# Loads and PSUM banks of the embedding start in a two-layer language-model tower

## Time and profile before

| | |
|---|---|
| Median of 3 runs | 4845.25 us (4837.85 to 4854.96) |
| Profiled execution, its own time | 4843.86 us |
| Its span | 4842.1 us |
| Mean granted TensorE clock | 0.96 of full |
| Busy share PE, DVE, ACT, POOL | 90%, 70%, 49%, 66% |

### The profile page before, as it was taken

How to read it: one execution, slowest core, us unless ns; L and a number is a source line. 1 busy time by engine, 2 the same in 40 slices (tenths; PEclk the granted TensorE clock), 3 DMA queues, 4 the chain that set the end, 5 groups by cost and what they waited for, 6 DMA issues and landing times. The chain is left out here.

```text
span 4842.1 us, 62755 instructions
## 1 busy us (share of the span) xinstructions
PE 4357.8 (90%) x17088; PEld 2261.8 (47%) x17088; DVE 3396.1 (70%) x5016; ACT 2378.6 (49%) x4078; POOL 3186.6 (66%) x1637
## 2 busy tenths in 40 slices
PE   6999986997899999999999999999999975999994
PEld 4666654664333333343433334343333333666673
DVE  4766673111799999999999999999999985111114
ACT  2555542222566665656666565666656534221221
POOL 2222212441799999999999999999999961444441
PEclk9999997998899999999999999999999987999997
DMA  1000012342223232323233333223323221333456
GB/s 31 20 23 20 20 49 60 112 126 73 97 100 106 102 106 99 105 99 104 100 105 103 101 105 100 102 100 108 105 103 105 96 76 38 103 117 112 125 167 219
DMA packets 262442, 453.11 MB, mean 94 GB/s; under 512 B 38892, under 2 KB 175932, under 8 KB 262300
## 3 DMA queue, kind: packets, MB, share of 16 engines
q1 hardware_dynamic: 238876, 403.66, 25.5%
q0 software_dynamic: 23424, 48.00, 3.2%
HBM read 409.75 MB, written 41.81 MB: 93 GB/s over the span
## 5 line engine op out<-in xcount | busy, mean ns | idle before, releaser
L1745 POOL TENSOR_TENSOR m_xh<-m_u,m_Bb 128x1536 f32<-128x1536 f32 x512 | 1752.1, 3452 | 220.2 <-DVE m_u L1619 220.2
L1674 PE MATMUL bank<-m_xh,ident 128*128 128x512 f32 x3072 | 1442.7, 605 | 25.2 <-POOL m_xh L1734 25.2
L1701 ACT ACTIVATE bank<-m_dt,m_Ac 128x508 f32<-128x508 f32 x1536 | 1019.2, 683 | 419.3 <-DVE bank L1716 283.6
L1716 DVE TENSOR_TENSOR_SCAN bank<-bank,m_xh 128x512 f32<-128x512 f32 x864 | 1060.1, 1227 | 36.3 <-ACT bank L1701 7.8
L1674 PEld LDWEIGHTS bank<-m_xh,ident 128*128 128x128 f32 x3072 | 567.7, 191 | 804.9 <-issue 732.6
L1716 DVE TENSOR_TENSOR_SCAN m_xh<-bank,m_xh 128x512 f32<-128x512 f32 x672 | 774.2, 1204 | 31.6 <-ACT bank L1701 27.3
L1734 POOL TENSOR_TENSOR m_xh<-m_xh,m_Cb 128x1536 f32<-128x1536 f32 x224 | 773.1, 3452 | 11.7 <-DVE m_xh L1716 11.3
L1725 DVE TENSOR_TENSOR m_xh<-bank,m_Cb 128x512 f32<-128x512 f32 x864 | 597.7, 692 | 70.0 <-DMA m_Cb<-BC_rows 24.9
L1184 ACT ACTIVATE f1t_h<-bank,f1t_b 128x512 f32<-128x512 f32 (+1 forms) x276 | 147.9, 587 | 509.9 <-PE bank L1214 491.1
L1533 PE MATMUL bank<-m_xp,m_dg 128*128 128x512 f32 x768 | 349.8, 598 | 3.3 <-ACT m_xc L1541 2.6
L1114 POOL DMA_INDIRECT rows_y<-f1t_y,f1t_home x142 | 140.1, 987 | 317.4 <-DVE f1t_y L1155 288.1
(11 more groups left out here) (366 smaller groups left out, 6142.6 us busy)
## 6 DMA issues: line engine op xcount, KB each, us to landing
m_Bb<-BC_rows SPq DMA_DIRECT2D x256, 512.0 KB, 4.7
m_Cb<-BC_rows SPq DMA_DIRECT2D x256, 512.0 KB, 3.9
f1t_w<-f_w SPq DMA_DIRECT2D x46, 576.0 KB
f1t_w1a<-f_w SPq DMA_DIRECT2D x46, 384.0 KB
f0t_w<-f_w SPq DMA_DIRECT2D x22, 576.0 KB
f1c_yg<-rows_y SPq DMA_DIRECT2D x16, 768.0 KB, 8.2
f1t_w1b<-f_w SPq DMA_DIRECT2D x92, 96.0 KB
f0t_w1a<-f_w SPq DMA_DIRECT2D x22, 384.0 KB
```

The source lines that it names most:

```text
L1674: mm = pe.matmul(bank[:, c, :], K.ident[:, :], xh[n % NX][:, c, :], start=False, stop=(d == 1 and n == NS - 1))
L1701: act.activation(o[:, :, lo:hi], seqs(dt[d][:, c, :])[:, :, lo:hi], ACT.Exp, scale=Ac[:, c, n:n + 1]).then_inc(s_dA, 1)
L1716: dve.tensor_tensor_scan(o, bank[:, 3 + p % 3, way], xh[n % NX][:, c, way], 0.0, ALU.mult, ALU.add).then_inc(s_h, 1)
L1745: pool.tensor_tensor(xh[n % NX][:, :, :], u[d][:, :, :], Bb[q % RB][:, n % QN, :].unsqueeze(1).to_broadcast([P, DC, TOK]), ALU.mult).then_ ...
```

## The change

Only the start of `attention_phase` is changed, and only for group 0; groups 1 to 15 keep their waits and bank 7.

- SP no longer waits for POOL in the load block. It issues `ids_w`, the three id rows of group 0 and the three tables, seven DMAs, each kind with a semaphore of its own, and waits for none of them. The id rows were issued in the main block before.
- The other 11 loads (gamma, beta and all weights) are issued by ACT at the beginning of the main block.
- The waits stand at the users: POOL's index copy waits for `ids_w`; PE's `emb0` for the tables; POOL's gamma step and PE's `q0` for all 11 weights.
- DVE sets the `V` tiles after the one-hots of group 0 instead of in the load block; ACT's first copy into `V` waits for it.
- The nine front steps of group 0 go to five banks (`BANKS`), and PE's waits between `emb0` and `emb1`, between `zT0` and `zT1` and between `q0` and `q4` are gone. Because banks 0 to 3 are among them, the first scores wait for the copies of all five of `q0` to `q4`.

```diff
+        WEIGHTS = (
+            (gam[:, :], ...), (bet[:, :], ...), (wqp_a ...), (wqp_b ...), (wqp_b bias ...),
+            (wq_a ...), (wq_b ...), (wq_b bias ...), (wo_a ...), (wo_b ...), (wo_b bias ...),
+        )
+        BANKS = {"emb0": 7, "emb1": 0, "zT0": 1, "zT1": 2, "q0": 3, "q1": 7, "q2": 0, "q3": 1, "q4": 2}
+        front = lambda g, name: BANKS[name] if isinstance(g, int) and g == 0 else FB
...
             @block.vector
             def _(dve):
-                for v in V:
-                    dve.memset(v[:, :, :, :], 0.0).then_inc(s_V, 1)
-                dve.wait_ge(s_V, 2)
-                for v in V:
-                    dve.memset(v[:, :, :, HD:HD + 1], 1.0)
...
             @block.sync
             def _(sp):
-                n = 0
-                sp.wait_ge(cleared, 4)
-                for dst, src in (
...
-                    (wo_b[CR:CR + 1, :], A["bproj"]), (ids_w[:, :], A["ids_wordT"]),
-                ):
-                    sp.dma_start(dst, src).then_inc(loaded, 16)
-                    n += 1
-                sp.wait_ge(loaded, 16 * n)
+                sp.dma_start(ids_w[:, :], A["ids_wordT"]).then_inc(s_idw, 16)
+                ids_front(sp, 0)
+                for dst, src in ((posi_t[:, :], A["posi_table"]), (ds_t[0:64, :], A["demo_table"]), (ds_t[64:66, :], A["seg_table"])):
+                    sp.dma_start(dst, src).then_inc(tables, 16)
...
             @block.sync
             def _(sp):
-                ids_front(sp, 0)
                 with sp.Fori(1, NG) as g:
                     ids_front(sp, g)
...
+                if isinstance(g, int) and g == 0:
+                    pool.wait_ge(s_idw, 16)
                 pool.tensor_copy(idx[:, :], ids_w[:, bass.ds(g * G, G)]).then_inc(s_idx, 1)
...
                 pool.wait_ge(s_xn, g * G + G)
+                if isinstance(g, int) and g == 0:
+                    pool.wait_ge(loaded, 16 * len(WEIGHTS))
...
+                    if not later:
+                        for v in V:
+                            dve.memset(v[:, :, :, :], 0.0).then_inc(s_V, 1)
+                        dve.wait_ge(s_V, 2)
+                        for v in V:
+                            dve.memset(v[:, :, :, HD:HD + 1], 1.0).then_inc(s_V, 1)
...
+            def act_loads(act):
+                for dst, src in WEIGHTS:
+                    act.dma_start(dst, src).then_inc(loaded, 16)
...
+                    if isinstance(g, int) and g == 0:
+                        act.wait_ge(s_V, 4)
...
@@ pe_embed
-                else:
+                    else:
+                        pe.wait_ge(tables, 48)
+                elif not isinstance(g, int) or g > 0:
                     pe.wait_ge(s_emb, g * 2 + 1)
...
@@ pe_q
                 if k == 0:
                     pe.wait_ge(s_zT, g * 2 + 2)
-                else:
+                    if isinstance(g, int) and g == 0:
+                        pe.wait_ge(loaded, 16 * len(WEIGHTS))
+                elif not isinstance(g, int) or g > 0:
                     pe.wait_ge(s_q, g * 5 + k)
...
@@ pe_scores
-                if j == 0:
+                if j == 0 and isinstance(g, int) and g == 0:
+                    pe.wait_ge(s_q, HC + 2)
+                elif j == 0:
                     pe.wait_ge(s_q, g * 5 + HC)
```

More of the change, by code:

```diff
@@ L177, in attention_phase @@
         loaded, cleared, mul3_set = sem("a_loaded"), sem("a_cleared"), sem("mul3_set")
+        s_idw, tables = sem("a_word_ids"), sem("a_tables")
         s_ids, s_idx, s_word = sem("ids_in"), sem("idx_ready"), *ctx.software(K, 1)
@@ L195, in attention_phase, with ids_front @@
         ACT_AT = {"keep": 10, "zT0": 10, "zT1": 11, "q0": 12, "q1": 12, "q2": 13, "q3": 14, "q4": 15}
+        WEIGHTS = (
+            (gam[:, :], A["ln_gamma"].partition_broadcast(P)), (bet[:, :], A["ln_beta"].partition_broadcast(P)),
+            (wqp_a[:, :].rearrange("p (h x) -> p h x", x=32)[:, :, 0:HD],
+             A["WqkvT"][0:P, 0:C].rearrange("k (h d) -> k h d", d=HD)),
+            (wqp_b[0:CR, :].rearrange("p (h x) -> p h x", x=32)[:, :, 0:HD],
+             A["WqkvT"][P:C, 0:C].rearrange("k (h d) -> k h d", d=HD)),
+            (wqp_b[CR:CR + 1, :].rearrange("p (h x) -> p h x", x=32)[:, :, 0:HD],
+             A["bqkv"][0:1, 0:C].rearrange("k (h d) -> k h d", d=HD)),
+            (wq_a[:, :], A["WqkvT"][0:P, 0:C]), (wq_b[0:CR, :], A["WqkvT"][P:C, 0:C]),
+            (wq_b[CR:CR + 1, :], A["bqkv"][0:1, 0:C]),
+            (wo_a[:, :], A["WprojT"][0:P, :]), (wo_b[0:CR, :], A["WprojT"][P:C, :]),
+            (wo_b[CR:CR + 1, :], A["bproj"]),
+        )
+        BANKS = {"emb0": 7, "emb1": 0, "zT0": 1, "zT1": 2, "q0": 3, "q1": 7, "q2": 0, "q3": 1, "q4": 2}
+        front = lambda g, name: BANKS[name] if isinstance(g, int) and g == 0 else FB
+        def ids_front(sp, g):
+            if not isinstance(g, int) or g > 0:
+                sp.wait_ge(s_onehot, g * 2)
+            sl = bass.ds(g * TOK, TOK)
+            sp.dma_start(pid[:, :], A["ids_posi"][sl].partition_broadcast(P)).then_inc(s_ids, 16)
+            sp.dma_start(did[0:64, :], A["ids_demo"][sl].partition_broadcast(64)).then_inc(s_ids, 16)
+            sp.dma_start(did[64:66, :], A["ids_seg"][sl].partition_broadcast(2)).then_inc(s_ids, 16)
         with nc.Block() as block:
@@ L337, in embed @@
                     dve.tensor_tensor(emb[:, 2 * b:2 * b + 2, :],
-                                      bank[:, FB, 0:2 * C].rearrange("p (j c) -> p j c", j=2),
+                                      bank[:, front(g, f"emb{b}"), 0:2 * C].rearrange("p (j c) -> p j c", j=2),
                                       word[:, 2 * b:2 * b + 2, :], ALU.add).then_inc(s_emb, 1)
@@ L420, in act_zT @@
                 if k == 0:
-                    act.copy(zTa[:, :], bank[:, FB, :]).then_inc(s_zT, 1)
+                    act.copy(zTa[:, :], bank[:, front(g, "zT0"), :]).then_inc(s_zT, 1)
                 else:
-                    act.copy(zTb[0:CR, :], bank[0:CR, FB, :]).then_inc(s_zT, 1)
+                    act.copy(zTb[0:CR, :], bank[0:CR, front(g, "zT1"), :]).then_inc(s_zT, 1)
             def act_q(act, g, i, k):
@@ L428, in act_q @@
                 if k < HC:
-                    act.copy(qT[i][:, k, :], bank[:, FB, :]).then_inc(s_q, 1)
+                    act.copy(qT[i][:, k, :], bank[:, front(g, f"q{k}"), :]).then_inc(s_q, 1)
                 else:
                     b = k - HC
+                    if isinstance(g, int) and g == 0:
+                        act.wait_ge(s_V, 4)
                     act.copy(V[i][:, 2 * b:2 * b + 2, :, 0:HD],
-                             bank[:, FB, 0:2 * C].rearrange("p (j h d) -> p j h d", j=2, h=HEADS)).then_inc(s_q, 1)
+                             bank[:, front(g, f"q{k}"), 0:2 * C].rearrange("p (j h d) -> p j h d", j=2, h=HEADS)).then_inc(s_q, 1)
             def act_exp(act, g, u):
@@ L471, in _ @@
             def _(act):
+                act_loads(act)
                 for step in ACT_STEPS.values():
@@ L481, in pe_embed @@
                         pe.wait_ge(s_q, g * 5)
-                else:
+                    else:
+                        pe.wait_ge(tables, 48)
+                elif not isinstance(g, int) or g > 0:
                     pe.wait_ge(s_emb, g * 2 + 1)
                 for j in (2 * b, 2 * b + 1):
-                    o = bank[:, FB, (j % 2) * C:(j % 2 + 1) * C]
+                    o = bank[:, front(g, f"emb{b}"), (j % 2) * C:(j % 2 + 1) * C]
                     sl = slice(j * P, (j + 1) * P)
@@ L498, in pe_zT @@
                 for j in range(G):
-                    o, v = (bank[:, FB, j * P:(j + 1) * P], z[:, j, 0:P]) if k == 0 else (bank[0:CR, FB, j * P:(j + 1) * P], z[:, j, P:C])
+                    f = front(g, f"zT{k}")
+                    o, v = (bank[:, f, j * P:(j + 1) * P], z[:, j, 0:P]) if k == 0 else (bank[0:CR, f, j * P:(j + 1) * P], z[:, j, P:C])
                     mm = pe.transpose(o, v, K.ident[:, :])
@@ L513, in pe_q @@
                     for j in (2 * (k - HC), 2 * (k - HC) + 1):
-                        o = bank[:, FB, (j % 2) * C:(j % 2 + 1) * C]
+                        o = bank[:, front(g, f"q{k}"), (j % 2) * C:(j % 2 + 1) * C]
                         sl = slice(j * P, (j + 1) * P)
```

13 lines of the change are left out of this document (1 added, 12 removed).

## The result

The changed kernel takes 4824.94 us (median of 7 runs, 4819.84 to 4826.67), against 4845.25 us for the kernel before, so the medians lie 20.3 us apart. The ratio is 0.9955 with a 95% interval of 0.9946 to 0.9964: 22 us saved, between 17 and 26. I had forecast 4825. Its profiled execution took 4824.94 us too, with a span of 4823.1.

The account below looks back on a forecast made before the run. The first 62.74 us were taken as one latency chain; load block 7.4, second embedding half 3.05, transposes 1.0, queries and values 3.1 and clock 6.0 sum to 20.6 us, giving 4823.3 profiled, 4825 median, range 4813 to 4838.

Parts of the forecast that it names:

- the two terms named for it: Lower end of the range, 4813: a cold stretch gone in group 1's front (4.5 us) and spread (5 us).
- The bound: First 62.74 us, to the first scores: pure latency, one chain of waiting engines; each microsecond taken comes off the end.
- Load block: Start of the kernel: SP's fewer issues and no wait for landings save 7.4 us, bounds 6.5 to 8.0.
- Gather: POOL's word-row gather, index copy to first addition: keeps its 9.4 us, so 0 gained or lost.
- my lower bound: Gather: 2.7 us lost if both V clearings, now beside it, count in full.
- Second half and transposes: Front: second embedding half saves 3.05 us with two banks; transposes save 1.0 us, all eight running directly on.
- Pauses: Queries and values, up to the mask: four pauses go, 0.98 us each, 3.9 us in all.
- The new wait: Before the mask of the first scores: waiting for the last V copy costs 0.8 us; net with pauses 3.1.
- Clock: Query run and mask: TensorE rises to 2.4 GHz 5 us into the run, saving 6.0 us, bounds 0 to 6.7.
- the step I gave a chance of 0.20 to fail: Rival on the query run: the clock stays low, 14.6 us saved, 4831; chance 0.20.
- Weights on ACT: Main block's start: ACT's 11 load issues, landed by 14 us, cost nothing, with 7 us of cover before POOL's gamma step.
- The rival: ACT issues dear: at 3.1 us per load the gain is gone, at 4.4 slower by 14.5 us; chance 0.04.

Follow-up runs that it names:

- the other kernels' marks: Three variants of the changed kernel: V cleared last (4828.24 us), front in banks 4 to 7 (4828.19 us), 14 unused matmuls ahead of the transposes (ratio 0.9953).
- the one-bank kernel: The changed kernel with group 0's front back in one PSUM bank and its waits of before, only the load order left; ratio 0.9993 (0.9982 to 1.0005).
- the 22 more loads: The changed kernel with 22 more small loads issued by ACT ahead of the weights; one execution 4845.11 us, then median 4831.55 us, ratio 0.9973.

## Why the prediction was right

**The time.** The median came within 0.1 us of the forecast, and that is luck: the saving is known only to 17 to 26 us. The lower end of my range, 4813, is 2.5 us below what the two terms named for it give (4825 less 4.5 and 5).

**The bound.** The front was one chain with nothing of another group beside it; the lead at the first scores, 19.97 us, was still 19.5 at 70 us, and 19.0 at the end. Behind the mask PE was less busy than I said, 30.9 of the 37.3 us from 62.74 to 100. That each microsecond "comes off the end" holds on the whole, not in each execution, as the other kernels' marks show.

**Load block.** Forecast 7.4, measured 7.29. The reason held: the block is SP's issue time, which moving the weights back onto SP showed (index copy at 12.72).

**Gather.** Forecast 0 between bounds of 1 gained and 2.7 lost, measured 0.15 lost. I had named the weight loads as a loss and the earlier id loads as a gain and sized neither. The weight loads cost 1.2 to 2.2 us (7.82 us without them), so something of about that size was gained, by my reading from the id loads. That the two cancelled is luck. The clearing, which set my lower bound, does not matter (9.00 and 9.05 us). The Trainium skill (SBUF — State Buffer, "SBUF: two separate sides") says that a gather's descriptors cannot be written while VectorE runs an operation that uses both ports; in this case the clearing showed no such loss.

**Second half and transposes.** 3.05 and 1.0 us forecast, 3.11 and 0.95 measured. PE's halves stayed under the gather.

**Pauses.** I counted more than PE's idle time because modelled ends overlap; 0.98 each. The new trace has 1.05 less from query step to query step (4.46 before, 33.84 to 37.25 now). The new wait cost 0.73 against my 0.8.

**Clock.** Forecast a rise 5 us in, measured 5.7, 5.5 us saved instead of 6.0. This was the step I gave a chance of 0.20 to fail. With the waits back it did stay low, so the dependence on the pauses is shown. That a pause-free stretch always lifts the clock is not: 5.8 us of it in the one-bank kernel did not, nor did 12.2 us in the earlier trace rows.

**Weights on ACT.** Their issue time was free, as forecast, though one issue took 2.08 us where the dearest row of before had 0.91. Their traffic was not: it is the 1.2 to 2.2 us of the gather above. Whether weights issued behind the gather would win that back is untested. The rival needed 3.1 us for each; the room it would have had to use up was some 6.7 us, and the 22 more loads measured it.

## What to carry to other kernels

When one stretch of a kernel is a chain, add its pieces from start times, not from idle times, and say of each edit what is late next; here that gave the sum within a microsecond of 20. Pauses between matmul steps cost twice: their own length, and a TensorE that stays at its low level (20.4 against 11.5 us for the same matmuls). And judge a change of a fraction of a per cent by marks in the trace near the edit, with the time of many runs only as the second witness.

## What was not expected of the hardware

- A DMA issue costs its queue 0.34 to 0.57 us for most loads here, but the bias load into the padded weight took 0.84 us on SP in the kernel before, 1.45 on SP behind other loads, and 1.89 to 2.12 on ACT.
- The same gather of four indirect DMAs took 7.8 us from index copy to first use with little beside it, and 9.0 to 10.4 beside other loads.
- The clock column reads 1.00 before the first recorded change, while the matmul durations say half of that (a pair of 512 columns 2.07 us against 1.13); only durations tell the level there.
- One execution met the low level more often in the Mamba stage (0.96 against 1.00 in one window of 370 us, by my estimate 14.8 us of work). It lost 15.2 us in that stage, three quarters of what this change brings.
